# ScalarE's order in an attention slot: the exponential ahead of the value copy and of the transposed-row copy

## The chip, the cores and the metric

The kernel runs on one core of one Trainium2 chip. The metric is device time in microseconds of one execution of the whole kernel; the lower the better. Times of several executions are summed up by their median.

## What is computed

The kernel is one transformer block on 16 batches of 256 tokens with 256 features, all in float32 at the interface:

```python
q = (layernorm(x) @ Wq_w + Wq_b)                      # 16 heads of 16 features
k = (ctx @ Wk_w + Wk_b); v = (ctx @ Wv_w + Wv_b)
scores = where(mask == 0, -1e9, q @ k.T / sqrt(16))
x = x + softmax(scores) @ v @ Wo_w + Wo_b
h = layernorm(x)
# feed-forward: 8 experts, the 2 best of each token, weighted by softmax(h @ gate_w.T)
out = sum over the 2 experts of w * ((silu(g) * u) @ down) + sigmoid(h @ sg) * shared_mlp(h)
return x + out
```

## The kernel before

**Stages.** The program has an attention stage (up to about 395 us of the profile; it also computes the router and rounds the expert weights into pairs of 16-bit parts), and a feed-forward stage that begins to fill TensorE towards the end of the first. The change is in the first alone.

**Slots.** Attention is a software pipeline written out by hand: iterations `i` of 8 slots `u`, the same nested loop in the instruction stream of each engine. In every slot TensorE issues, in this order: the scores S of one unit (batch `i-1`, unit `u`; a unit is a query half and a group of 4 heads' pairs; lines 1101 masks and 1120 products), the ring work of the slot, the transposed scores T of one unit of an earlier batch (lines 1101 and 1136), and in every other slot the product with the values PV (line 1152). S units go to one PSUM pair `ps_st`, T units to the other. VectorE takes the row maximum of each S (line 994); ScalarE takes the exponential of each T (line 803). The next S waits for the maximum of the last S, and the next T waits for the exponential of the last T, because each pair is used again at once (`wait_pair`).

**The ring.** Projections and transposes share two PSUM banks `ps_m` in turn. The steady order of a period is: slot 0 `mt` (transposed maxima, line 1281) and `rt` (router, line 1418), slot 1 `xt`, slot 2 `ct` (transposes, line 1162), slot 3 `q`, slot 4 `k` (projections, line 1175), slot 5 `v` (value projection, line 1311), slot 6 `ht` (transposes of the normalised rows of batch `i-5`, line 1409), slot 7 `o` (output projection, line 1251). Whoever writes a bank waits until its last user has freed it, so `o` waits for the copy of `v`, and `mt` for the copy of `ht`.

**ScalarE.** In slot 5 ScalarE before the change waits for the value projection, makes two copies of it into `vx` (line 776, 128x256 each), waits for their own semaphore, frees the bank, and then waits for the T unit of the slot and takes its exponential (line 803). In slot 6 it does the same with one copy of the transposed rows into `hT` (line 745, 128x1024 of 16 bits) ahead of the exponential. From slot 4 it carries two copies of the attention output out of `ps_o` (lines 814 and 815) and two DMA issues for the sums (line 377, `sums_across`). The first of the copies waits until GpSimd has divided the outputs of the batch before (line 655, semaphore `s_n`). The buffer `vx` has three parts, used by batch modulo 3; PV of a batch needs its values two iterations after they are projected. The rows `hT` are read by the router in slot 0 of the next iteration and by a DMA (line 824) that ScalarE issues after the exponential of slot 7.

**Other queues.** SyncE's queue carries, in order, the load of the context, the loads of expert weights (line 498), the writes (519) and reads (531, 532) of `q` and `k` through DRAM, and the joining of the sums (383), which waits for the sums DMA of ScalarE. In iterations 5 to 9 there is a second load of expert weights behind the join. GpSimd rounds the weights (631, 638), scatters rows (1393) and divides (655, 663). On VectorE slots 5 and 6 hold the routing chain (1334 to 1348), the maximum of S, the normalisation (871, 877), and in slot 7 a reciprocal (935), a maximum, and the residual add (1010).

Below, units are named by slot: T5 is the T unit of slot 5, PE issues it behind the value projection; T6 is that of slot 6 and waits for the exponential of T5; S7 is the scores unit of slot 7.

Of the kernel before, what the change touches and what calls it, by code (L numbers as in the profile page):

```python
# [5 lines left out]
FP16 = mybir.dt.float16  # L6
# [8 lines left out]
D = 256  # L15
NB = 16
# [149 lines left out]
def attention(nc, sb, sem, xr, fwh, fwl, ident, moe, x, ctx, mask, w_in, bias_in, w_o, ffn_in, gate_in, ident_in,  # L166
# [4 lines left out]
    with ExitStack() as here:  # L171
# [131 lines left out]
        def now(kind, i, u):  # L303

            return [b for b in range(NB) if when.get((kind, b)) == 8 * i + u]
# [121 lines left out]
        def taken(i, u, kind):  # L427

            g = 8 * i + u
            found = filler.get(g - 1) if g <= LAST_T + 1 else filler.get(g)  # L430
            return found[1:] if found and found[0] == kind else None
# [253 lines left out]
        def _(eng):  # L685
# [24 lines left out]
            def shared_high(n, c):  # L710
# [7 lines left out]
                    eng.wait_ge(s_st, 8 * (NB - 1)) if n else eng.wait_ge(s_v, NB)  # L718
                eng.activation(f_hi[n % 2][rows, c, :], hf[k % 2][rows, :], ACT.Copy).then_inc(moe.f_hh, 1)

            eng.wait_ge(s_anyb, 1)
            eng.activation(anyr[:, :], bank("any")[:, 0:SEQ], ACT.Copy).then_inc(s_any33, 1)
            eng.wait_ge(s_any33, 1)
# [3 lines left out]
            for i in range(ITER):  # L727
                for u in range(8):
# [8 lines left out]
                        eng.wait_ge(s_small, 64)  # L737
                        eng.activation(gh[:, :, :], g32[:, :, :], ACT.Copy).then_inc(s_gh, 1)
                    for kind, b in uses(i, u):
                        if kind == "ht":  # L740
                            eng.wait_ge(s_ht, b + 1)
                            if b:
                                eng.wait_ge(s_rt, b)
                                eng.wait_ge(s_tw, 16 * b)
                            eng.activation(hT[:, :, :, :].rearrange("p l c t -> p (l c t)"),
                                           bank((kind, b))[:, :].bitcast(FP16), ACT.Copy).then_inc(s_th, 1)
                            eng.wait_ge(s_th, b + 1)
                            eng.nop().then_inc(free((kind, b)), 1)
                        elif kind == "mt":
                            eng.wait_ge(s_mt, b + 1)  # L750
                            if b:
                                eng.wait_ge(s_mw, 16 * b)
                            eng.activation(nm[:, :], bank((kind, b))[0:H, 0:SEQ], ACT.Copy, scale=-1.0).then_inc(s_nm, 1)
                            eng.wait_ge(s_nm, b + 1)
                            eng.nop().then_inc(free((kind, b)), 1)
                        elif kind in ("xt", "ct"):
                            s_in, dst, s_out, s_used = (s_xt, xT[0], s_xh, s_q) if kind == "xt" else (s_ct, cT[0], s_ch, s_v)
                            eng.wait_ge(s_in, b + 1)
                            if b:
                                eng.wait_ge(s_used, b)  # L760
                            eng.activation(dst[:, :], bank((kind, b))[:, :], ACT.Copy).then_inc(s_out, 1)
                        elif kind in ("q", "k"):
                            s_in, dst, s_out, s_used = (s_q, qhl, s_qh, s_qw) if kind == "q" else (s_k, khl, s_kh, s_kw)
                            eng.wait_ge(s_in, b + 1)
                            if b:
                                eng.wait_ge(s_used, 16 * b)
                            eng.activation(dst[:, :, 0, :], bank((kind, b))[:, :].rearrange("p (h t) -> p h t", h=2),
                                           ACT.Copy).then_inc(s_out, 1)
                        elif kind == "v":
                            eng.wait_ge(s_v, b + 1)  # L770
                            if b == 0:
                                eng.wait_ge(s_const, 7)
                            if b >= 3:
                                eng.wait_ge(s_pv, 4 * (b - 2))
                            for tt in range(TT):
                                last = eng.activation(vx[b % 3][:, tt, :, 0:DK],
                                                      bank((kind, b))[:, tt * D:(tt + 1) * D].rearrange("p (h d) -> p h d", h=H),
                                                      ACT.Copy)
                                last.then_inc(s_vx, 1)
                            eng.wait_ge(s_vx, 2 * b + 2)  # L780
                            eng.nop().then_inc(free((kind, b)), 1)  # L781
                    if (i, u) == (0, 2):
                        eng.wait_ge(s_bias, 32)
                        eng.wait_ge(s_ones, 1)
# [11 lines left out]
                    if st:  # L796
                        n = 8 * st[0] + st[1]
                        eng.wait_ge(s_st, n + 1)
                        if n >= 4:
                            eng.wait_ge(s_pv, (n - 4) // 2 + 1)  # L800
                        if n == 3:
                            eng.wait_ge(s_gl, 1)
                        eng.activation(expo[n % 4][:, :, :], ps_st[pair["T", n]][:, :].rearrange("p (h q) -> p h q", h=4), ACT.Exp,  # L803
                                       scale=SCALE).then_inc(s_e, 1)
                    if taken(i, u, "up"):
                        shared_high(*taken(i, u, "up"))
                    if pv and pv[1] == 7:
# [1183 lines left out]
```

## Time and profile before

| what | value |
|---|---|
| median of 3 runs | 814.75 us |
| the runs | 810.08, 815.7, 814.75 us |
| span of the profiled execution | 811.5 us |
| time of the profiled execution apart from its span | not listed |
| TensorE busy | 744.4 us, 92% of the span |
| ScalarE busy | 397.1 us, 49% |
| VectorE busy | 547.1 us, 67% |
| GpSimd busy | 340.9 us, 42% |
| mean granted TensorE clock | 0.977 of full |

The span runs from the first to the last instruction of one profiled execution. It lies inside the range of the three timed runs.

### The profile page before, as it was taken

The page shows a single profiled execution, that of the slowest core. Times are in us where ns is not written, and L with a number is a line of the kernel's source. Part 1 is how long each engine was busy: PE and PEld are TensorE (multiplying, and loading weights), DVE is VectorE, ACT ScalarE, POOL GpSimd, SP SyncE. Part 2 cuts the span into 40 slices and gives each one's busy share as a digit, 9 for nine tenths or more (in the row PEclk, how much of TensorE's full clock was granted, in tenths as well). Part 3 has the DMA queues.
Part 4 walks back from the last instruction along what each step waited for, and adds up shares of the span by engine and source line. Part 5 has one row for each costly group of instructions (what it writes and reads, how often), then busy time and mean ns, then how long its engine had stood idle before and what let it go on. Part 6 is the DMA issues. An engine that isn't in the chain of part 4 may idle for free.

```text
span 811.5 us, 21926 instructions
## 1 busy us (share of the span) xinstructions
PE 744.4 (92%) x8123; PEld 464.9 (57%) x8123; DVE 547.1 (67%) x1174; ACT 397.1 (49%) x679; POOL 340.9 (42%) x499
## 2 busy tenths in 40 slices
PE   5689899989988999998989978999999999999997
PEld 4445455545555555554454654677777777655555
DVE  6675677978988998888765678533333333358797
ACT  4124556655655666666555462344444444433231
POOL 6131144586676665555403232011121121267773
PEclk9878999999999999999999999999999999999999
DMA  6643555655554554545512213488888988834743
GB/s 185 174 135 122 169 153 168 184 157 164 158 140 139 165 152 150 155 132 162 152 42 75 86 60 111 102 168 176 168 164 175 162 165 172 153 115 124 234 148 113
DMA packets 164234, 118.26 MB, mean 146 GB/s; under 512 B 108450, under 2 KB 143522, under 8 KB 164132
## 3 DMA queue, kind: packets, MB, share of 16 engines
q1 hardware_dynamic: 146564, 82.44, 41.3%
q0 software_dynamic: 9552, 26.10, 10.7%
q10 hardware_dynamic: 8016, 8.33, 3.3%
q8 instruction: 69, 1.13, 0.6%
q14 instruction: 33, 0.27, 0.1%
HBM read 52.78 MB, written 38.14 MB: 112 GB/s over the span
## 4 chain that ended last, share of the span: by engine, by line
PE 52%; DVE 14%; DMA 9%; POOL 7%; ACT 7%; issue 6%; SPq 4%; ACTq 1%; DVEq 0%; POOLq 0%
PE ps_st L1889 15%; PE ps_m L1904 8%; PE ps_st L1461 5%; PE ps_st L1101 5%; DVE mx L994 4%; PE ps_o L1152 4%; PE ps_m L1175 3%; POOL p L1670 2%; POOL expert_rows L1393 2%; DMA arena<-ffn_dram 2%; PE ps_st L1120 2%; PE ps_m L1251 2%; ACT p L803 2%; PE ps_o L1472 1%; DMA qk_scratch<-arena 1%
## 5 line engine op out<-in xcount | busy, mean ns | idle before, releaser
L994 DVE TENSOR_REDUCE mx<-ps_st 128x4 f32<-128x1024 f32 x128 | 155.7, 1217 | 40.2 <-PE ps_st L1120 32.5
L803 ACT ACTIVATE p<-ps_st 128x1024 f32<-128x1024 f32 x128 | 131.0, 1023 | 75.8 <-PE ps_st L1136 68.1
L1889 PE MATMUL ps_st<-fwh,p 128*128 x568 | 137.9, 313 | 1.1 <-DMA p<-expert_rows 1.1
L1662 POOL DMA_DIRECT2D sorted_out<-p x71 | 38.6, 543 | 180.7 <-ACT p L1719 177.0
L1393 POOL DMA_INDIRECT expert_rows<-hrow,slot x64 | 64.7, 1011 | 59.4 <-DVE slot L1384 38.7
L1889 PE MATMUL ps_st<-fwl,p 128*128 x284 | 88.8, 313 | 0.0
L1889 PEld LDWEIGHTS ps_st<-fwh,p 128*128 128x128 f16 x568 | 55.5, 98 | 28.3 <-issue 2.0
L1101 PE MATMUL ps_st<-maskq,identb 64*64 64x512 bf16 x512 | 53.8, 410 | 19.5 <-DVE mx L994 15.3
L1101 PE MATMUL ps_st<-mb_k,identb 64*64 64x512 bf16 x256 | 52.4, 406 | 18.9 <-ACT p L803 18.1
L1461 PE MATMUL ps_st<-qk,arena 128*128 128x512 f16 x264 | 61.1, 386 | 3.3 <-DVE qk L913 1.8
L1461 PE MATMUL ps_st<-q,arena 128*128 128x512 f16 x264 | 59.7, 379 | 3.2 <-DVE qk L913 2.2
L1719 ACT ACTIVATE p<-ps_m 128x256 f32<-128x256 f32 x71 | 27.2, 383 | 69.8 <-PE ps_m L1904 67.2
L1670 POOL DMA_INDIRECT p<-sorted_out,xn x52 | 53.0, 1019 | 17.8 <-issue 14.6
L631 POOL CAST fwh<-arena 128x272 f16<-128x272 f32 x80 | 33.5, 459 | 63.3 <-DMA arena<-ffn_dram 63.3
L1811 DVE TENSOR_TENSOR qk<-ps_st,maskq 128x352 f32<-128x352 f32 x36 | 18.9, 524 | 60.5 <-PE ps_st L1889 60.3
L1811 DVE TENSOR_TENSOR qk<-ps_st,vx 128x352 f32<-128x352 f32 x35 | 18.4, 524 | 59.8 <-PE ps_st L1889 59.8
L1175 PE MATMUL ps_m<-arena 128*128 128x256 f16 x256 | 54.2, 285 | 0.5 <-ACTq L781 0.4
L638 POOL TENSOR_TENSOR fwl<-arena,fwh 128x272 f16<-128x272 f32 x80 | 54.2, 710 | 0.6
L1101 PE MATMUL ps_st<-turned_k,identb 64*64 64x512 bf16 x256 | 52.4, 406 | 0.0
L1152 PE MATMUL ps_o<-p,vx 128*17 128x256 f32 x704 | 48.7, 396 | 0.0
L1101 PEld LDWEIGHTS ps_st<-maskq,identb 64*64 64x64 bf16 x512 | 14.7, 105 | 56.8 <-DVE mx L994 36.9
L1461 PEld LDWEIGHTS ps_st<-qk,arena 128*128 128x128 f16 x264 | 25.3, 99 | 34.7 <-issue 3.0
(237 smaller groups left out, 1750.4 us busy)
## 6 DMA issues: line engine op xcount, KB each, us to landing
arena<-ffn_dram SPq DMA_DIRECT2D x20, 544.0 KB
sorted_out<-p POOLq DMA_DIRECT2D x71, 128.0 KB, 2.9
qk_scratch<-arena SPq DMA_DIRECT2D x32, 256.0 KB, 2.9
qk<-qk_scratch SPq DMA_DIRECT2D x44, 128.0 KB, 3.0
arena<-ctx_dram SPq DMA_DIRECT2D x16, 256.0 KB, 3.8
hT_dram<-hT ACTq DMA_DIRECT2D x16, 256.0 KB, 2.5
out_dram<-xr SPq DMA_DIRECT2D x16, 256.0 KB, 2.9
xr<-x_dram SPq DMA_DIRECT2D x7, 512.0 KB, 4.2
```

Source lines behind the costliest of these rows:

```text
L638: last = eng.tensor_tensor(lo[:, cols], aw32[:, cols], hi[:, cols], ALU.subtract)
L803: eng.activation(expo[n % 4][:, :, :], ps_st[pair["T", n]][:, :].rearrange("p (h q) -> p h q", h=4), ACT.Exp, scale=SCALE).then_inc(s_e, 1)
L994: eng.tensor_reduce(mx[b % 2][:, qt, :].rearrange("p (h g j) -> p h g j", h=2, g=HG)[:, :, hg, :], ps_st[pair["S", 8 * b + n]][:, :].rearr ...
L1101: mm(ps[to, 2 * hh * SEQ:2 * (hh + 1) * SEQ], identb[rows, rows], bias[rows, :].unsqueeze(1).broadcast_to([64, 2, SEQ]), start=True, stop= ...
L1152: last = mm(ps_o[32 * j:32 * j + DK + 1, hg * SEQ:(hg + 1) * SEQ], vx[b % 3][:, kt, 4 * hg + j, :], expo[(8 * b + 2 * hg + kt) % 4][:, 2 * ...
L1175: mm(oo, w[:, at:at + P], srcT[xl][:, dc * SEQ:(dc + 1) * SEQ], start=dc == 0 and (wl, xl) == TERMS[0], stop=False)
L1393: eng.indirect_dma_start(expert_rows, bass.IndirectOffsetOnAxis(moe.slot[:, j, n:n + 1], 0), hrow[:, tt, :], None).then_inc(moe.s_sc[b % 3 ...
L1461: last = eng.matmul(o[:, :], moe.sw[:, wl, at:at + P], moe.hT[blk % 2][:, :, xl, dc, :], start=dc == 0 and (wl, xl) == (0, 0), stop=dc == ...
L1662: eng.dma_start(sorted_out[k * P:(k + 1) * P, :], ys[k % 3][:, :]).then_inc(r_st[k % 3], 16)
L1670: eng.indirect_dma_start(ya[n % NGB][:, j, :], None, sorted_out, bass.IndirectOffsetOnAxis(packed[:, j, n:n + 1], 0)).then_inc(r_ga[n % NG ...
L1889: last = mm(o[:, 0:INTER], xgT[k % NXG][:, xl, dc, :], (fwh, fwl)[wl][:, bass.ds(e, 1), w0 + dc * INTER:w0 + (dc + 1) * INTER], start=dc = ...
L1904: last = mm(ps_d[2 + b % 2][:, 0:D], turned(b)[:, xl, c, :], (fwh, fwl)[wl][:, bass.ds(e, 1), at:at + D], start=c == 0 and (wl, xl) == (0, ...
```

## The change

In slots where batch 3 or a later one has its value projection, the two copies of the values, with the wait for the projection and the release of the bank, move behind the exponential of the slot. In iterations below 16 the copy of the transposed rows, with its waits and its release, moves behind the exponential of its slot too. Batches 0 to 2 keep the old order for the values, and iterations 16 on keep it for the rows (batch 11 and later). No instruction is added or removed; the two blocks became functions. The DMA issues of ScalarE and its other work keep their places behind both.

```diff
+            def values_out(b):
+                eng.wait_ge(s_v, b + 1)
+                ...
+                if b >= 3:
+                    eng.wait_ge(s_pv, 4 * (b - 2))
+                for tt in range(TT):
+                    last = eng.activation(vx[b % 3][:, tt, :, 0:DK], ..., ACT.Copy)
+                    last.then_inc(s_vx, 1)
+                eng.wait_ge(s_vx, 2 * b + 2)
+                eng.nop().then_inc(free(("v", b)), 1)
+
+            def turned_rows_out(b):
+                eng.wait_ge(s_ht, b + 1)
+                if b:
+                    eng.wait_ge(s_rt, b)
+                    eng.wait_ge(s_tw, 16 * b)
+                eng.activation(hT[:, :, :, :].rearrange("p l c t -> p (l c t)"),
+                               bank(("ht", b))[:, :].bitcast(FP16), ACT.Copy).then_inc(s_th, 1)
+                eng.wait_ge(s_th, b + 1)
+                eng.nop().then_inc(free(("ht", b)), 1)
...
                     for kind, b in uses(i, u):
-                        if kind == "ht":
-                            ...
+                        if kind == "ht" and i >= NB:
+                            turned_rows_out(b)
...
-                        elif kind == "v":
-                            ...
+                        elif kind == "v" and b < 3:
+                            values_out(b)
...
                         eng.activation(expo[n % 4][:, :, :], ps_st[pair["T", n]][:, :].rearrange("p (h q) -> p h q", h=4), ACT.Exp,
                                        scale=SCALE).then_inc(s_e, 1)
+                    for b in now("v", i, u):
+                        if b >= 3:
+                            values_out(b)
+                    for b in now("ht", i, u):
+                        if i < NB:
+                            turned_rows_out(b)
                     if taken(i, u, "up"):
```

## Rows read from the trace of the kernel before

**Rows 1.** The page: the chain that ended last, shares by engine

```profile
PE 52%; DVE 14%; DMA 9%; POOL 7%; ACT 7%; issue 6%; SPq 4%; ACTq 1%; DVEq 0%; POOLq 0%
```

**Rows 2.** Waits of TensorE, 80 to 375 us: total, times, longest

```profile
PE ps_st L1101 <- ACT p L803: 16.6, 14, 3.7
```

**Rows 3.** Timeline of batch 12's slots: start, length, engine, line, idle before

```profile
298.87 0.39 PE L1136 MATMUL ps_st<-qk 49*64 49x256 f16 x8
298.95 0.66 ACT L776 ACTIVATE vx<-ps_m 128x256 f32<-128x256 f32 x2 [0.78 <-PE ps_m L1311]
...
299.80 1.02 ACT L803 ACTIVATE p<-ps_st 128x1024 f32<-128x1024 f32 x1 [0.19 <-ACT vx L776]
...
300.71 1.02 ACT L745 ACTIVATE hT<-ps_m 128x1024 f16<-128x1024 f16 x1
300.83 1.21 DVE L994 TENSOR_REDUCE mx<-ps_st 128x4 f32<-128x1024 f32 x1
...
300.87 0.40 PE L1101 MATMUL ps_st<-mb_k,identb 64*64 64x512 bf16 x2 [0.62 <-ACT p L803]
...
302.42 0.41 PE L1101 MATMUL ps_st<-maskq,identb 64*64 64x512 bf16 x4
...
303.29 1.16 DVE L994 TENSOR_REDUCE mx<-ps_st 128x4 f32<-128x1024 f32 x1
...
304.61 0.41 PE L1101 MATMUL ps_st<-mb_k,identb 64*64 64x512 bf16 x2
304.72 0.69 DVE L1010 TENSOR_TENSOR xr<-ps_m,xr 128x512 f32<-128x512 f32 x1 [0.27 <-PE ps_m L1251]
```

**Rows 4.** The chain that ended last, 40 to 400 us: start, length, what

```profile
81.78 0.67 ACT vx L776 x2
...
201.22 3.58 DMA sums<-odd
...
367.52 0.67 ACT vx L776 x2
```

**Rows 5.** Timeline of batch 7's slots 4 to 7, from 174 us

```profile
174.67 0.60 ACT L814 ACTIVATE oj<-ps_o 128x512 f32<-128x512 f32 x1 [3.08 <-POOL rb L655]
...
177.04 0.66 ACT L776 ACTIVATE vx<-ps_m 128x256 f32<-128x256 f32 x2 [0.77 <-issue]
177.89 1.02 ACT L803 ACTIVATE p<-ps_st 128x1024 f32<-128x1024 f32 x1 [0.19 <-ACT vx L776]
...
178.96 0.40 PE L1101 MATMUL ps_st<-mb_k,identb 64*64 64x512 bf16 x2 [3.71 <-ACT p L803]
...
184.28 0.40 PE L1101 MATMUL ps_st<-mb_k,identb 64*64 64x512 bf16 x2
```

**Rows 6.** Timeline: T5 and T6 of batch 3, T6 of batches 4, 9 and 10

```profile
81.15 0.39 PE L1136 MATMUL ps_st<-qk 49*64 49x256 f16 x8
...
83.70 0.40 PE L1101 MATMUL ps_st<-mb_k,identb 64*64 64x512 bf16 x2 [1.72 <-ACT p L803]
...
106.49 0.40 PE L1101 MATMUL ps_st<-mb_k,identb 64*64 64x512 bf16 x2 [1.17 <-ACT p L803]
...
229.36 0.40 PE L1101 MATMUL ps_st<-mb_k,identb 64*64 64x512 bf16 x2 [2.50 <-ACT p L803]
...
253.83 0.40 PE L1101 MATMUL ps_st<-mb_k,identb 64*64 64x512 bf16 x2 [2.05 <-ACT p L803]
```

**Rows 7.** Stretches: length, busy of five engines, granted TensorE clock, DMA, GB/s

```profile
86.00:88.00 2.00, 1.92 (x28) 0.92 (x24) 0.78 (x1) 0.03 (x1) 0.00 (x0) 0.58 0.26 57
...
181.00:183.00 2.00, 2.00 (x21) 1.02 (x18) 0.77 (x1) 0.03 (x1) 0.39 (x1) 0.50 0.46 68
...
226.00:232.00 6.00, 3.50 (x65) 1.87 (x58) 5.47 (x15) 4.28 (x7) 5.33 (x10) 1.00 0.63 140
...
256.00:258.00 2.00, 2.00 (x18) 1.07 (x11) 1.13 (x1) 0.00 (x0) 0.21 (x1) 0.50 0.22 49
```

**Rows 8.** Batch 13: the first scores unit of the next iteration

```profile
328.43 0.41 PE L1101 MATMUL ps_st<-maskq,identb 64*64 64x512 bf16 x4 [0.45 <-DMA qk<-qk_scratch]
```

More of the change, by code:

```diff
@@ L719, in shared_high @@
                 eng.activation(f_hi[n % 2][rows, c, :], hf[k % 2][rows, :], ACT.Copy).then_inc(moe.f_hh, 1)
+            def values_out(b):
+                eng.wait_ge(s_v, b + 1)
+                if b == 0:
+                    eng.wait_ge(s_const, 7)
+                if b >= 3:
+                    eng.wait_ge(s_pv, 4 * (b - 2))
+                for tt in range(TT):
+                    last = eng.activation(vx[b % 3][:, tt, :, 0:DK],
+                                          bank(("v", b))[:, tt * D:(tt + 1) * D].rearrange("p (h d) -> p h d", h=H),
+                                          ACT.Copy)
+                    last.then_inc(s_vx, 1)
[10 more added lines that the diff above has]
+                eng.nop().then_inc(free(("ht", b)), 1)
             eng.wait_ge(s_anyb, 1)
@@ L739, in _ @@
                     for kind, b in uses(i, u):
-                        if kind == "ht":
[L741 to L748, printed above, removed]
+                        if kind == "ht" and i >= NB:
+                            turned_rows_out(b)
                         elif kind == "mt":
@@ L768, in _ @@
                                            ACT.Copy).then_inc(s_out, 1)
-                        elif kind == "v":
[L770 to L781, printed above, removed]
+                        elif kind == "v" and b < 3:
+                            values_out(b)
                     if (i, u) == (0, 2):
```

## The prediction

> **What bounds the kernel now.** I read the page first. Its busy times say that TensorE is occupied for 92% of the span (the table above has it), and the chain by engine gives it only 52%, with 7% on ScalarE [rows 1]. So the end is set by TensorE with hand-overs to the other engines in between, and an edit of ScalarE's order can pay only at such a hand-over. The second view is the waits of TensorE in the stretch where the edit acts: 16.6 us of idle time before a T unit ended with an exponential, 14 times, the longest 3.7 us [rows 2]. These 16.6 us are the whole pot in which the change can fish. The third view is the timeline of one ordinary batch, and it shows where in the period the hand-over is: T6 starts at 300.87 after 0.62 us of idle time, right behind the end of T5's exponential at 299.80 + 1.02 = 300.82 [rows 3]. That exponential was itself late: T5's last products end at 298.87 + 0.39 = 299.26, but ScalarE was in the two value copies until 298.95 + 0.66 = 299.61 and then waited 0.19 us for its own semaphore [rows 3]. The fourth view is the chain that ended last. It passes through the value copies of eight batches, the first at 81.78 (batch 3) and the last at 367.52 (batch 15); the others are 4, 7, 10, 11, 12 and 14 [rows 4]. It goes round those of 5, 6, 8, 9 and 13, by a DMA or by SyncE's queue, as at 201.22 where the sums transfer of batch 8 carries it [rows 4].
>
> **The value copies, in ordinary batches (4, 11, 12, 14, 15).** Nothing is added or removed; two copies, one self-wait and one release go from before the exponential to behind it. In batch 12 the exponential would start when T5 has landed, estimated at 299.26 + 0.05 = 299.31 (the 0.05 is a hand-over between the two engines: in batch 7 the exponential ended at 178.91 and TensorE went on at 178.96 [rows 5]). Before, it started at 299.80, so it is 0.49 us earlier, and T6 starts at 300.38 with 0.13 us of idle time left [rows 3]. Does the 0.49 reach the end? First limit: S7 needs the maximum of S6, which VectorE begins only at 300.83, behind its routing chain, and ends at 302.04 [rows 3]. S7 stood at 302.42, so it can come 0.33 earlier (302.04 + 0.05 = 302.09), and then VectorE is late, not ScalarE. Second limit: the residual add at 304.72 waited 0.27 us for TensorE; VectorE is free for it at 303.29 + 1.16 = 304.45 [rows 3]. From there the chain runs on VectorE (the add, statistics, the maximum of the next S). So 0.27 us of the 0.49 are kept. Bounds: zero, if a loop beside this chain is just behind it, and 0.49. I take 0.27, since it is read off a row. Five batches: 5 x 0.27 = 1.35 us.
>
> **The value copies where GpSimd held ScalarE (batches 7 and 10).** In batch 7 ScalarE stood for 3.08 us before a slot 4 copy until GpSimd had divided [rows 5]. T5 was complete long before, so here the exponential takes the place of the value copies at once: 177.04 in place of 177.89, which is 0.85 us, and the pause of TensorE before T6 falls from 3.71 to 2.86 [rows 5]. No limit behind it is near: T6 comes so late there that VectorE has long ended the maximum of S6. Batch 10 has the same pattern with a pause of 2.05 us [rows 6]. Two batches: 1.70 us. Batch 9 has it too (2.50 us [rows 6]) but the chain goes round it: GpSimd, the sums transfer and the next load of expert weights form a loop of their own there, and an earlier T6 only lengthens the next pause. I count nothing for 8 and 9.
>
> **Batch 3.** ScalarE came to the value copies only at 81.78 [rows 4], later than T5 ended (81.15 + 0.39 = 81.54 [rows 6]), so the exponential takes their place at once and again the whole 0.85 us is won. Its pause of 1.72 us [rows 6] becomes 0.87.
>
> **Batches 5, 6 and 13.** After batch 13 the first scores unit waited 0.45 us for the read of q and k from DRAM [rows 8]. That transfer starts from slot 3 and 4, ahead of the edit. A T6 that comes 0.3 us earlier only lengthens this wait. Nothing for these three.
>
> **The transposed rows.** The copy of 1.02 us at 300.71 ran before T6's exponential, which waited for it until 301.91 [rows 3]. Now the exponential starts at about 301.2 and the copy ends near 303.3 in place of 301.73. The next T unit, which needs that exponential, comes at 304.61 [rows 3], so the gain is worth nothing. The delay is covered as well: the bank goes to the transposed maxima and the rows to the router, both behind 304.61, so about 1.3 us of cover are left. The DMA of the rows is issued after the exponential of slot 7, behind 305, and is not moved. If that cover were gone the cost would be up to the 1.02 + 0.19 us of the copy and its wait in each of the 11 iterations.
>
> **What the later value copies cost.** They now end at 300.34 + 0.66 = 301.0, and the bank is free at about 301.2 in place of 299.8. Who is queued for it is the output projection, behind S7 at 302.42, or at 302.09 when S7 comes earlier [rows 3]: at least 0.9 us of cover. In batch 7 the release comes near 178.9 and that projection stands beyond 181, so there is more. PV of that batch comes two iterations later. ScalarE's DMA issues of slot 4 stand ahead of slot 5 and are not moved, those of slot 7 stand behind its exponential; SyncE's and GpSimd's queues are passed by nothing. Taken at zero.
>
> **TensorE's clock.** Behind the pause of batch 7 the granted clock fell: 0.50 of full, the 1.2 GHz level, from 181 to 183, and T6 to the next T took 184.28 - 178.96 = 5.32 us [rows 5, 7] against 304.61 - 300.87 = 3.74 in batch 12 [rows 3]. One such fall costs 1.58 us. A fall came after the pauses of 3.71, 2.05 and 1.72 us (0.50, 0.50 and 0.58 of full), and none after that of 2.50 (1.00) [rows 5 to 7]. So a shorter pause may avoid it, but the length alone doesn't decide. I take the falls of 7 and 10 as kept, since the one pause stays long and the other is lengthened again by what batch 9 gives it, and that of batch 3 as gone, since its pause is halved. There I count 0.4 us, not 1.58, because the next scores then wait for the reads of q and k. Bounds of this term: 0 to 2 x 1.58 + 0.4 = 3.6 us in favour, and as much against if other pauses are now followed by a fall. The Trainium skill (TensorE: Matmul & The Clock Gate, section "What's actually happening") says that the gate judges recent activity over a window that runs freely and is not started by the kernel; by this rule the 2.50 us pause without a fall beside the 2.05 us one with a fall is a matter of phase, and every shift of the schedule draws anew. The sum by it would be the same 3.9 us plus or minus a draw; the trace agrees as far as these four pauses go.
>
> **Sum.** 1.35 + 1.70 + 0.85 + 0.4 = 4.3 us, 0.5% of the span of 811.5. The profiled execution's time apart from its span isn't listed; the span lies inside the three runs (810.08 to 815.7), 3.25 below their median. I subtract from the median: 814.75 - 4.3 = 810.4 us. The shift should reach the end, since the chain behind attention is TensorE for most of its length.
>
> **Rivals.**
> First, the gain is lost: the chain goes through the value copies only by small margins, and the loops beside it (SyncE's reads and weight loads, GpSimd's rounding) are a fraction of a microsecond behind, as in 5, 6, 8, 9 and 13. For it: rows 8, and the loop in batches 8 and 9. Against it: batches 11, 12 and 14 repeat without any such wait. If only 3, 7 and 10 pay half, 1.3 us: 813.5.
> Second, the gain is larger, because the clock no longer falls after batches 7 and 10: 4.3 + 2 x 1.58 = 7.5 us: 807.3. For it: the pause of 2.05 us gets shorter. Against it: 2.86 us is still long. To get over 1%, which is 8.1 us and about what a measurement of this kernel can tell from no change, this would have to come with the full 0.49 in the ordinary batches (5 x 0.22 = 1.1 more): 806.2.
> Third, it becomes slower: the clock falls more often. The place is the pauses before T6 that remain (batches 4, 7, 8, 9, 10), the price is 1.58 us for each new fall, and it decides from three new falls on, since 3 x 1.58 = 4.7 is more than 4.3. Four new ones: 814.75 - 4.3 + 6.3 = 816.8. For it: a fall came after 1.72 us but not after 2.50, and batch 4's pause of 1.17 isn't much shorter [rows 6]. Against it: all pauses get shorter or stay.
> Fourth, the change doesn't do what it says: in one place the exponential isn't earlier, since T5 lands after the value copies. In batch 12 T5 ended at 299.26 and the copies at 299.61 [rows 3], so this holds only if TensorE gets later relative to ScalarE: 814.75.
>
> **How the numbers follow.** Forecast 0.52; gain lost 0.20; larger 0.15; slower 0.08; without effect 0.05. The range reaches to the larger case's 806.2 and takes in the lost and the void one: 805.5 to 815.5, since the three runs alone lie 5.6 apart. Faster by over 1% (below 806.6): 0.10. Slower by over 1% (above 822.9): 0.03. Within 1%: 0.87.
>
> **What would show it.** In the timeline of the changed kernel the exponential of T5 starts within 0.1 us of the end of T5 and the value copies follow; the idle time before T6 is 0.1 to 0.2 us in ordinary batches, and in batches 7 and 10 about 0.85 less than before if their length is otherwise kept. The exponentials' share in TensorE's waits falls from 16.6 us to about 9. S7 begins within 0.1 us of the end of S6's maximum. In the chain the pair of value copy and exponential is replaced by the maximum of S6. The granted clock from 84 to 88 us stays at 1.00. The forecast is wrong if the output projection or the router waits for a ScalarE copy, if the ordinary batches keep their period, or if falls of the clock multiply.

## The result, and the profile after

| | before | after |
|---|---|---|
| median of 16 runs each, taken together | 810.01 us | 803.25 us |
| lowest and highest run | 807.02, 815.7 | 800.67, 809.49 |
| profiled execution: its time, its span | not listed, 811.5 | 800.67, 798.5 |
| mean granted TensorE clock | 0.977 | 0.984 |

The ratio is 0.9911, 95% interval 0.9892 to 0.9931: 0.9% faster, 7.2 us of 810. The same kernel measured a second time (e8 below) gave 0.9937 [0.991, 0.9963], 5.1 us. The gain is therefore told as 5 to 7 us, from two measurements whose intervals together reach from 3 to 9 us. The forecast was 4.3 us of gain and 810.4 us; the time fell outside its range on the fast side. The two profiled executions lie 13.0 us apart, about twice the gain of the medians, so they can't be subtracted from each other as they stand. This is taken up below.

First the chain that ended last, by engine, as the page of the changed kernel has it:

```profile
PE 48%; DVE 25%; issue 7%; DMA 7%; POOL 6%; ACT 4%; SPq 2%; DVEq 0%; ACTq 0%; POOLq 0%
```

Against [rows 1] ScalarE fell from 7% to 4% and VectorE rose from 14% to 25%: the hand-over that the edit shortened is now passed on VectorE. TensorE's waits from 80 to 375 us say the same (total, times, longest):

```profile
PE ps_st L1115 <- DVE mx L1008: 8.2, 22, 1.4
PE ps_st L1115 <- ACT p L811: 6.9, 5, 2.9
PE ps_st L1115 <- DMA qk<-qk_scratch: 1.6, 3, 1.0
```

The 16.6 us in 14 waits of [rows 2] became 6.9 in 5. Next, the timeline of batch 12, which answers to [rows 3]:

```profile
287.94 0.39 PE L1150 MATMUL ps_st<-qk 49*64 49x256 f16 x8
...
288.38 1.02 ACT L811 ACTIVATE p<-ps_st 128x1024 f32<-128x1024 f32 x1 [1.14 <-PE ps_st L1150]
288.58 2.68 POOL L638 TENSOR_TENSOR fwl<-arena,fwh 128x272 f16<-128x272 f32 x4
...
288.73 0.59 DVE L1359 TENSOR_TENSOR chosen<-which,table 128x32 f32<-128x32 uint32 x1
289.30 0.66 ACT L729 ACTIVATE vx<-ps_m 128x256 f32<-128x256 f32 x2
289.36 0.61 DVE L1362 TENSOR_TENSOR sel<-chosen 128x16 f16<-128x16 f32 x1
...
289.45 0.40 PE L1115 MATMUL ps_st<-mb_k,identb 64*64 64x512 bf16 x2
...
289.89 1.21 DVE L1008 TENSOR_REDUCE mx<-ps_st 128x4 f32<-128x1024 f32 x1
...
291.06 1.02 ACT L742 ACTIVATE hT<-ps_m 128x1024 f16<-128x1024 f16 x1
291.16 0.41 PE L1115 MATMUL ps_st<-maskq,identb 64*64 64x512 bf16 x4
...
292.35 1.16 DVE L1008 TENSOR_REDUCE mx<-ps_st 128x4 f32<-128x1024 f32 x1
...
293.35 0.41 PE L1115 MATMUL ps_st<-mb_k,identb 64*64 64x512 bf16 x2
293.46 0.69 DVE L1024 TENSOR_TENSOR xr<-ps_m,xr 128x512 f32<-128x512 f32 x1
```

T5 ends at 287.94 + 0.39 = 288.33 and its exponential starts 0.05 later; the value copies follow; T6 starts at 289.45 with no idle time, 0.05 behind the exponential. S7 starts 0.06 behind the end of S6's maximum (289.89 + 1.21 = 291.10), and the residual addition no longer waits for TensorE: it starts right behind VectorE's own maximum, where it waited 0.27 us before. The copy of the rows ends at 292.08, with 1.27 us left until T7. From residual addition to residual addition an ordinary batch takes 22.40 us in place of 22.72 to 22.75. (Batch 14, with a wait for the read of q and k in it, takes 22.59 in place of 23.13.)

The places with a pause, in batches 3, 7, 9 and 10, answer to [rows 5] and [rows 6]:

```profile
79.21 0.40 PE L1115 MATMUL ps_st<-mb_k,identb 64*64 64x512 bf16 x2 [0.87 <-ACT p L811]
...
168.16 0.60 ACT L828 ACTIVATE oj<-ps_o 128x512 f32<-128x512 f32 x1 [3.07 <-POOL rb L655]
...
170.53 1.02 ACT L811 ACTIVATE p<-ps_st 128x1024 f32<-128x1024 f32 x1 [0.77 <-issue]
171.45 0.66 ACT L729 ACTIVATE vx<-ps_m 128x256 f32<-128x256 f32 x2
171.60 0.40 PE L1115 MATMUL ps_st<-mb_k,identb 64*64 64x512 bf16 x2 [2.86 <-ACT p L811]
...
176.92 0.40 PE L1115 MATMUL ps_st<-mb_k,identb 64*64 64x512 bf16 x2
...
220.72 0.41 PE L1115 MATMUL ps_st<-mb_k,identb 64*64 64x512 bf16 x2 [1.64 <-ACT p L811]
...
244.80 0.40 PE L1115 MATMUL ps_st<-mb_k,identb 64*64 64x512 bf16 x2 [1.32 <-ACT p L811]
...
248.55 0.40 PE L1115 MATMUL ps_st<-mb_k,identb 64*64 64x512 bf16 x2
```

The pauses before T6 were 1.72, 3.71, 2.50 and 2.05 us and are 0.87, 2.86, 1.64 and 1.32. In 3 and 7 that is 0.85 less each, the length of the value copies with their wait, as forecast. The stretches, whose last figures are granted clock, DMA share and GB/s, show what the clock did behind batches 3 (first two rows), 7 and 10, against [rows 7]. The fall of batch 3 stood 2.3 us behind the start of its T6 before (83.70), so it is to be looked for from 81 us on, and not only from 84:

```profile
81.00:83.00 2.00, 1.02 (x28) 0.63 (x24) 1.22 (x1) 1.02 (x1) 0.00 (x0) 1.00 0.33 84
84.00:88.00 4.00, 3.82 (x70) 1.87 (x63) 2.65 (x4) 2.70 (x4) 0.00 (x0) 1.00 0.45 139
172.00:174.00 2.00, 2.00 (x40) 0.73 (x28) 0.35 (x1) 1.82 (x3) 2.00 (x4) 0.73 0.17 53
174.00:176.00 2.00, 2.00 (x17) 1.20 (x10) 1.23 (x1) 0.22 (x1) 0.79 (x2) 0.50 0.22 49
246.00:250.00 4.00, 4.00 (x69) 2.58 (x62) 3.79 (x7) 2.19 (x3) 1.96 (x4) 1.00 0.24 53
```

Behind batch 7 it still fell to 0.50, the 1.2 GHz level, and T6 to T7 took 176.92 - 171.60 = 5.32 us, as before. Behind 3 and 10 it stayed at 1.00: T6 to T7 took 2.01 us in batch 3 (before 3.26) and 3.75 in batch 10 (before 5.31).

**Where the profile pair's 13.0 us lie.** Subtracting the starts of the residual additions gives a shift that grows step by step. 3.64 us of it stood already at 68 us, ahead of the first instruction that the edit moves, under the same instruction order in both kernels: that part isn't the change's. (The first residual addition comes in batch 4's slots, so the part of batch 3 is read from TensorE's next S units: 88.59 and 82.81, a shift of about 5.8.) From there to 361 us the shift grows by 8.80 to 12.44, and then it stays, to the last addition of attention at 455.83 (12.47). So what was won in attention did reach the end. By batches:

| batches | forecast | grown in the pair |
|---|---|---|
| 3 | 0.85 + 0.4 | 2.15 |
| 4, 11, 12, 14, 15 | 1.35 | 1.99 |
| 7, 10 | 1.70 | 0.43 + 1.95 |
| 5, 6, 13 | 0 | 1.01 |
| 8, 9 | 0 | 0.33 + 0.94 |
| sum | 4.3 | 8.80 |

### The profile page after: what moved, and what is told of

Read it like the earlier page. It is cut to its first block, busy times and chain, and to the rows that moved or that the text cites. A ratio compares the mean times of both kernels' runs of the same rounds, so it can differ in the third digit from the quotient of the medians.

```text
span 798.5 us, 21926 instructions
## 1 busy us (share of the span) xinstructions
PE 739.3 (93%) x8123; PEld 463.8 (58%) x8123; DVE 548.0 (69%) x1174; ACT 395.8 (50%) x679; POOL 339.5 (43%) x499
## 4 chain that ended last, share of the span: by engine, by line
PE 48%; DVE 25%; issue 7%; DMA 7%; POOL 6%; ACT 4%; SPq 2%; DVEq 0%; ACTq 0%; POOLq 0%
PE ps_st L1903 16%; DVE mx L1008 9%; PE ps_m L1918 8%; PE ps_st L1475 5%; PE ps_st L1115 4%; POOL p L1684 3%; PE ps_o L1166 2%; DMA qk_scratch<-arena 2%; PE ps_m L1189 2%; POOL expert_rows L1407 2%; PE ps_st L1134 2%; PE ps_o L1486 1%; DVE arena L1064 1%; PE ps_m L1486 1%; DVE arena L1058 1%
## 5 line engine op out<-in xcount | busy, mean ns | idle before, releaser
L1733 ACT ACTIVATE p<-ps_m 128x256 f32<-128x256 f32 x71 | 27.2, 383 | 69.5 <-PE ps_m L1918 67.0
L1475 PEld LDWEIGHTS ps_st<-qk,arena 128*128 128x128 f16 x264 | 25.4, 99 | 35.1 <-issue 3.9
```

What stands on the lines that cost most here:

```text
L1475: last = eng.matmul(o[:, :], moe.sw[:, wl, at:at + P], moe.hT[blk % 2][:, :, xl, dc, :], start=dc == 0 and (wl, xl) == (0, 0), stop=dc == ...
```

## The experiments

Each builds on the changed kernel. In all, the two conditions (`b >= 3` for the values, `i < NB` for the rows) are written as lists of batches, which give the changed kernel for 3 to 15 and 0 to 10. Ratios are to the kernel before on the same chip; it had a median of 811.54 us on the chip of e1 to e4, 853.27 on that of e5 to e7, 810.34 on that of e8 to e11 and 812.14 on that of e12. Each experiment has one profiled execution.

**e1_values_only and e2_rows_only: one part alone.**

```diff
-ROWS_LATE = tuple(range(0, 11))      # e1
+ROWS_LATE = ()
-VALUES_LATE = tuple(range(3, 16))    # e2
+VALUES_LATE = ()
```

> Only the value copies (batches 3 to 15) go behind the exponential; the transposed rows keep the old order. Theory A (all of the gain comes from an earlier exponential of T5; the rows' order is worth nothing because T7 comes more than 3 us later): the whole gain of the change stays, 6 to 8 us, ratio 0.990 to 0.993, and in batch 12 TensorE waits at most 0.15 us before T6. Theory B (the rows' order carries a part, by freeing T6's exponential or by unloading VectorE's and ScalarE's PSUM reads): at least 2 us of the gain are missing, ratio 0.994 or above.

> Only the copy of the transposed rows (batches 0 to 10) goes behind its exponential; all value copies keep the old order. Theory A: nothing, within 1 us of the kernel before, ratio 0.999 to 1.001, and in batch 12 T6 still waits 0.62 us. Theory B: 2 us or more faster, ratio 0.9975 or below. If the later release of the bank or of the rows holds the router up, it is slower by up to 1.2 us in each of 11 iterations.

Measured: e1 0.9916 [0.9884, 0.9948], e2 0.9991 [0.996, 1.0023]. The values alone carry the whole gain, as theory A has it. The rows alone do nothing that can be seen: the interval would hide up to 3 us, but in e2's profile the ordinary batches keep their 22.7 us (two of them have 23.1, like batch 14 before) and T6 of batch 12 still waits 0.63 us.

**e3_ordinary and e4_held: the values in two groups of batches.**

```diff
+VALUES_LATE = (4, 5, 6, 8, 11, 12, 13, 14, 15)   # e3
+VALUES_LATE = (3, 7, 9, 10)                      # e4
```

> Value copies go behind the exponential only in the batches where ScalarE wasn't held before them (4, 5, 6, 8, 11 to 15), rows as in the change. Theory A: about 0.33 us for each of the ordinary batches that lie on the chain, the limit being VectorE's maximum of S6; 7 to 9 of them, 2.3 to 3.0 us, ratio 0.996 to 0.997; the pauses of batches 3, 7, 9, 10 keep their length (1.7, 3.7, 2.5, 2.0 us). Rival (the gain is mostly the ordinary batches, my 0.27 us having been too low because the limit behind it moves too): 5 us or more, ratio 0.994 or below.

> Value copies go behind the exponential only in batches 3, 7, 9 and 10, where the exponential could take their place at once; rows as in the change. Theory A: 0.85 us in each of 3, 7 and 10 and, where the shorter pause spares a fall of TensorE's clock, 1.25 us (batch 3) and 1.56 us (batch 10) more: 2.5 us if no fall is spared, 5.4 us if both are, ratio 0.997 to 0.993; the granted clock behind batch 10's pause is 1.00. Rival (the falls are chance and don't hang on the length of these pauses): 2.5 us, ratio 0.997, with falls in some pauses of this profile as in the one before.

Measured: e3 0.9973 [0.9942, 1.0004], e4 0.9953 [0.9923, 0.9983], 2.2 and 3.8 us. e4 alone is clear of no change; e3 isn't. Together they make 0.74%, near e1's 0.84%. Both lie in theory A's ranges. e3 has the short period (22.41) in batches 11, 14 and 15 (12 and 13 take 23.07, which is taken up under e8), and yet in batch 7 this:

```profile
174.09 0.64 PE L1117 MATMUL ps_st<-mb_k,identb 64*64 64x512 bf16 x2 [4.20 <-ACT p L813]
...
180.20 0.40 PE L1117 MATMUL ps_st<-mb_k,identb 64*64 64x512 bf16 x2
```

The pause that was 3.71 us is 4.20 there: TensorE comes earlier, GpSimd's division doesn't, and 0.49 us of what batches 4 to 6 won is given back. The fall behind it cost more too (6.11 us from T6 to T7). The pauses of batches 9 and 10 did not keep their length either: they were 2.02 us, now with a fall (T6 to T7 5.18), and 0.60, without one.

**e5_route_later: VectorE's routing of batches 0 to 9 a slot later,** so that S6's maximum no longer stands behind it.

```diff
+when.update({("route", b): 8 * (b + 6) + 6 for b in range(10)})
```

> The changed kernel, and VectorE's routing chain of batches 0 to 9 goes from slot 5 to slot 6, behind the maximum of S6 in place of ahead of it. Theory A (after the change VectorE is the limit of the ordinary batches: the maximum of S6 waits for the routing chain, and S7 for that maximum): S7 no longer waits, up to 0.16 us more in each of 10 iterations, but the chain's 2.2 us still stand before the maximum of S7 and the residual add; so between 1.6 us faster and 1 us slower than the change alone, ratio to the kernel before 0.989 to 0.9925. Rival (VectorE isn't the limit, the hand-over of T6 still is): ratio as the change's 0.991 within 0.0005 and S7 stands where it stood. If the chain now delays the residual add by its whole length, up to 2 us in each iteration are lost and the kernel is slower than before.

Measured: 0.9998 [0.997, 1.0026], so it loses the gain, as the last sentence of the expectation feared. The distance between residual additions of batches 11 to 14 is 25.4 to 25.8 us, but for one of 27.2, with 24.5 for e6 on that chip. S7's wait is gone, but the addition now comes 1.53 us behind T7 in place of 0.11, since the routing stands ahead of it, and other maxima are late: from 80 to 400 us TensorE waits for maxima 33 times, 15.9 us in all, where e6 has 21 and 9.7. The profiled execution was one of e5's longest (860.58 us, median 853.15), so the 0.9 to 1.3 us of the distances are no typical size; the ratio doesn't rest on it.

**e6_keep_busy and e9_busy_once: no fall of the clock by keeping TensorE busy.** In the pause TensorE repeats the transposes of slot 6 (the same result again): in e6 for three batches, in e9 for the iteration of batch 7 alone.

```diff
-transpose_rows(eng, moe, bank((kind, b)), hrow[b % 3]).then_inc(s_ht, 1)
+for _ in range({2: 5, 4: 3, 5: 3}.get(b, 0)):    # e6; e9: 3 if b == 2 else 0
+    transpose_rows(eng, moe, bank((kind, b)), hrow[b % 3])
+transpose_rows(eng, moe, bank((kind, b)), hrow[b % 3]).then_inc(s_ht, 1)
```

> The changed kernel, and TensorE repeats the transposes of the rows in the pauses before T6: 5 more times for the rows of batch 2 (pause of value batch 7, 2.86 us), 3 more times for those of 4 and 5 (batches 9 and 10, 1.64 and 1.32 us). The repeats write the same values to the same bank. Theory A (the clock falls behind a pause because TensorE did too little before): with about 0.45 us for each repeat the clock behind batch 7's pause stays at 1.00, T6 to T7 takes 3.9 us in place of 5.3, and 1.4 to 1.6 us are gained on the change: ratio 0.989 to 0.9905 to the kernel before. Rival (falls come by chance or by something else, such as power or a fixed time in the kernel): the fall behind batch 7 stays, T6 to T7 is 5.3 us, ratio as the change's.

> The changed kernel, and TensorE repeats the transposes of the rows 3 more times in the pause before T6 of value batch 7 alone (about 0.45 us each, inside a pause of 2.86 us, so that T6 isn't delayed). Theory A (the fall behind that pause is caused by TensorE's idleness): T6 to T7 takes 3.75 to 3.9 us in place of 5.3, the clock from there on is 1.00, and 1.4 us are gained on the change, ratio lower by 0.0017. Rival (the fall comes whatever TensorE does there): 5.3 us again, ratio as e8's.

Measured: e6 0.9936 [0.9904, 0.9967], e9 0.9941 [0.9912, 0.9971]; the change itself has 0.9937 on e9's chip. In both profiles the fall of batch 7 is gone (T6 to T7 3.75 and 3.74). e9's stretches there:

```profile
170.00:172.00 2.00, 1.39 (x28) 0.63 (x28) 1.35 (x3) 1.82 (x4) 2.00 (x4) 1.00 0.41 119
172.00:174.00 2.00, 2.00 (x30) 1.42 (x25) 1.16 (x1) 1.23 (x2) 1.80 (x4) 1.00 0.22 49
```

The total shows nothing of it, so the first half of theory A held and its gain didn't. In e6 the repeats were too many: T6 of batches 9 and 10 started 1.2 us behind the end of T5's exponential. In e9, T6 to T7 of batch 9 took 8.01 us in place of 3.74, for another reason:

```profile
215.13 1.29 POOL L665 TENSOR_TENSOR onl<-rb,onh 128x256 f16<-128x256 f32 x2
215.28 3.84 DVE L1354 TENSOR_TENSOR sc<-ex,tot 128x16 f32<-128x16 f32 x1
216.39 2.67 POOL L640 TENSOR_TENSOR fwl<-arena,fwh 128x272 f16<-128x272 f32 x4
...
220.15 1.22 DVE L1010 TENSOR_REDUCE mx<-ps_st 128x4 f32<-128x1024 f32 x1
...
221.42 0.41 PE L1117 MATMUL ps_st<-maskq,identb 64*64 64x512 bf16 x4 [3.04 <-DVE mx L1010]
```

A routing operation of 16 elements a partition, usually 0.28 us, took 3.84, and its end (219.12) is that of GpSimd's row of subtractions (219.06). The maximum behind it is late, and S7 waits 3.04 us. The loss isn't 4.3 us, though: in return the pause of batch 9 is 0.49 us in place of 1.64 and that of batch 10 is gone, so the two batches take 50.20 us together, against 48.72 in the first profile of the change. And over batches 7 to 10 e9 takes 98.79 us against 98.91, in spite of the fall that it was spared. e4 has 98.73 there and no profile has less. So something behind TensorE seems to hold these four batches together; which engine it is was not tried here.

**e7_values_slot6 and e10_values_slot6_again: the value copies still later,** behind the exponential of slot 6. This tests how much cover the ring leaves.

```diff
-for b in now("v", i, u):
-    if b in VALUES_LATE:
+for b in range(NB):
+    if when.get(("v", b)) == 8 * i + u - 1 and b in VALUES_LATE:
```

> The changed kernel, and the value copies of batches 3 to 15 move one slot further, behind the exponential of T6. This takes the cover of the bank's release away. Theory A (the cover is about 0.9 us before the output projection): the bank is free near 0.85 us after the end of T6's exponential, some 0.3 us later than the output projection wants it, so that projection waits for a ScalarE copy and 0.2 to 0.4 us are lost in each of 8 to 10 batches: 2 to 4 us slower than the change, ratio 0.993 to 0.996. Rival (the output projection has slack of its own, since VectorE is the limit now): ratio as the change's 0.991.

> The changed kernel with the value copies behind the exponential of T6, one slot further, now beside the change on one chip. Theory A (the later value copies cost nothing as long as the bank is free before the output projection; at 2.7 us after T5's exponential they end just as it comes): within 1 us of e8, the output projection starts at most 0.1 us later. Rival (the bank's release has less cover than the trace shows): 2 us or more slower than e8.

Measured: e7 0.9914 [0.9885, 0.9942], e10 0.9936 [0.9909, 0.9963], the latter beside 0.9937 for the change on that chip. In e7 the output projection is now behind the copies, by hardly anything:

```profile
305.21 0.66 ACT L731 ACTIVATE vx<-ps_m 128x256 f32<-128x256 f32 x2
...
305.96 0.10 PEld L1263 LDWEIGHTS ps_m<-bhl,tri 128*128 128x128 f16 x1 [0.25 <-ACTq L736]
```

So the cover of the ring was real: a further slot of delay costs nothing that the total can show. It isn't nothing in the profiles: T6 to T7 takes 3.99 us in both, against 3.90 in e8 and 3.94 in e6 on the same chips, and an undisturbed batch of e10 takes 22.50 us where the change has 22.40, so the cover ends here.

**e8_change_again: the changed kernel once more.**

> The changed kernel itself once more, beside the three that follow, since the last three ran on a chip where the kernel before takes 853 us. Theory A (the gain is made of ScalarE's hand-overs and of spared falls of the clock, which any chip has): ratio 0.989 to 0.993. Rival (part of the gain belongs to the chip or to the state in which the program starts): ratio above 0.995.

Measured: 0.9937 [0.991, 0.9963], 804.7 us beside 810.34, between the two theories' ranges, and its interval takes in parts of both. In its profile batch 10 pauses for 2.38 us and the clock falls behind it (T6 to T7 5.31), where the first profile had 1.32 and no fall; batch 7 pauses for 3.36. Batches 12 and 14 take 23.06 and 24.19 us where the first profile had 22.40 and 22.59:

```profile
291.60 0.64 DVE L1352 TENSOR_TENSOR sc<-ex,tot 128x16 f32<-128x16 f32 x1
...
295.40 0.41 PE L1117 MATMUL ps_st<-maskq,identb 64*64 64x512 bf16 x4 [0.74 <-DVE mx L1010]
...
321.81 0.41 PE L1117 MATMUL ps_st<-maskq,identb 64*64 64x512 bf16 x4 [1.18 <-DMA qk<-qk_scratch]
```

The routing operation `sc` took 0.64 us in place of 0.28, since it started beside another of GpSimd's operations (see the last section), and S7 waited 0.74 us for the maximum behind it. Such batches of 0.66 us more, with T6 to T7 at 4.56, come seven times in the profiles of e1, e3, e8 and e10, six of them with a `sc` of 0.58 to 0.65, and not at all in the first profile. In batch 14 the read of q and k was 1.18 us late on top, where the first profile had 0.23. From the addition of batch 4 to that of batch 15 the same program took 256.78 us in one execution and 261.40 in the other.

**e11_outputs_behind: in iterations 7, 9 and 10 the output copies, the sums DMAs and the copy for the division go behind the exponential of slot 5,** so that it no longer waits for GpSimd.

```diff
-if pv and pv[1] == 7:
+if pv and pv[1] == 7 and i not in (7, 9, 10):
     outputs_out(pv[0])
...
+if i in (7, 9, 10) and u == 5:
+    outputs_out(units(i, 4)[2][0])
+    divide(i, 4)
```

> A version built on the reading that the pauses left before T6 (2.86, 1.64 and 1.32 us in batches 7, 9 and 10) come from ScalarE standing in its slot 4 copies until GpSimd has divided: in iterations 7, 9 and 10 those copies, the copy of the divided outputs and the two DMA issues go behind T5's exponential too. Theory A: T6 no longer pauses there, TensorE stops later at PV, which needs the outputs out of PSUM, but T6 and its exponential are done by then; 1.0 to 2.5 us in batch 7, 0.5 to 1.5 in 9 and 10, and the fall behind batch 7 may go (1.5 more): 2 to 5 us faster than e8, ratio 0.984 to 0.989. Rival (GpSimd's loop sets the pace there, so a pause moves from T6 to PV one for one): within 1 us of e8.

Measured: 0.992 [0.9886, 0.9954], 805.12 us, not clearly better than the change's 0.9937, and short of theory A. The pauses of 7, 9 and 10 are gone, and two costs stand in their place. In batch 7:

```profile
173.58 0.40 PE L1129 MATMUL ps_st<-mb_k,identb 64*64 64x512 bf16 x2
...
174.65 1.06 PE L1180 MATMUL ps_o<-p,kv 128*17 128x256 f32 x16 [0.44 <-ACT odd L732]
...
176.72 0.27 PE L1275 MATMUL ps_m<-bhl,tri 128*128 128x256 f16 x1 [0.45 <-POOL onl L665]
```

T6 starts unhindered, but PV waits for the bank of the outputs and the output projection for GpSimd: T6 to T7 takes 4.76 in place of 3.74. And batch 8, which had no pause, now has the one that batch 7 lost:

```profile
196.61 0.60 ACT L731 ACTIVATE oj<-ps_o 128x512 f32<-128x512 f32 x1 [3.06 <-POOL rb L657]
...
200.06 0.57 PE L1129 MATMUL ps_st<-mb_k,identb 64*64 64x512 bf16 x2 [2.85 <-ACT p L841]
```

Over batches 7 to 10 this profile (one of the longer executions, 809.34 us) takes 105.08 us, against 102.03 in e8. So the wait for GpSimd's division only moved to the next batch: ScalarE's order chose where TensorE stands still for it, here at a worse place.

**e12_routing_split: e9 with the last two operations of VectorE's routing (`chosen`, `sel`) behind the maximum of S6,** in the routing of batches 0 to 9.

```diff
-for _ in route(eng, link, moe, b, s_sel):
-    pass
+pieces = route(eng, link, moe, b, s_sel)
+next(pieces)
+next(pieces)
+halfway.append(pieces)
...
+if u == 6 and halfway:
+    for _ in halfway.pop():
+        pass
```

> The change with the repeats of e9_busy_once for rows of batch 2, and in the routing of batches 0 to 9 VectorE's last two operations of the chain (chosen, sel) are issued behind the maximum of S6 in place of before it. Theory A, VectorE's maximum is now the end that TensorE waits for in the ordinary batch: S7's wait for S6's maximum (0.16 us after the change) goes, the distance between residual additions of ordinary batches falls from 22.40 to between 22.1 and 22.25, and the ratio to before is 0.988 to 0.992. Theory B, VectorE's work per batch is the limit whatever its order: the distance stays 22.40 and the ratio is as e9_busy_once's, 0.993 to 0.995. In either case a stall of some us in one batch, as the 3.84 us operation of e9_busy_once, stays possible where VectorE's operations stand beside GpSimd's.

Measured: 0.9911 [0.9881, 0.9941], 803.32 us, on another chip than e9. The interval takes in e9's ratio and both theories'. The profile tells more. VectorE in the ordinary batch there:

```profile
291.19 0.64 DVE L1364 TENSOR_TENSOR sc<-ex,tot 128x16 f32<-128x16 f32 x1
...
292.55 1.22 DVE L1011 TENSOR_REDUCE mx<-ps_st 128x4 f32<-128x1024 f32 x1
...
293.87 1.04 DVE L893 TENSOR_SCALAR xn<-xr,mv,rsa 128x256 f32<-128x256 f32 x2
294.95 0.19 DVE L1373 TENSOR_TENSOR chosen<-which,table 128x32 f32<-128x32 uint32 x1
295.18 0.17 DVE L1376 TENSOR_TENSOR sel<-chosen 128x16 f16<-128x16 f32 x1
...
295.53 1.16 DVE L1011 TENSOR_REDUCE mx<-ps_st 128x4 f32<-128x1024 f32 x1
296.61 0.67 DVE L1027 TENSOR_TENSOR xr<-ps_m,xr 128x512 f32<-128x512 f32 x1
```

S7's wait is gone (T6 to T7 3.74 in place of 3.90), but the distance is 22.35 to 22.36, only 0.05 less than 22.40. The two moved operations became short (0.19 and 0.17 in place of 0.59 and 0.61), but in this batch `sc` took 0.64 in place of 0.28 and the normalisation 1.04 in place of 0.73, and the maximum of S7 and the addition still stand in a row behind them. The first half of theory A held, its gain didn't: in this part of the period VectorE's sum counts, as theory B has it. The stalled operation came again in batch 9 (3.83 us), and so did the clock's fall behind batch 7, after a pause of 2.00 us, in spite of the repeats.

## Why the prediction was wrong, step by step

The mechanism was right. Three terms were mis-sized: the base that the gain was subtracted from (4.74 us too high), the clock (0.4 us, where the profile pair has 2.8 and the average over executions about 1.3), and the batches that were given nothing (2.28 us in the pair). They stand one by one below, with two smaller ones.

**The base.** Of the 7.15 us between the forecast and the median, 4.74 are the step "I subtract from the median: 814.75". That was the middle of three runs 5.6 us apart; 16 runs have 810.01. The ratio that the forecast implies, 0.53% off, lies just outside the interval of the first measurement (0.69% to 1.08%) and inside that of the repeat (0.37% to 0.90%).

**The direction, the mechanism and the place were right.** The exponential of T5 starts 0.05 us behind T5, T6 has no idle time in ordinary batches, the waits for exponentials fell from 16.6 to 6.9 us (forecast about 9; 9.3 in e8), no engine waits for a moved copy, and the values alone give the whole effect (e1, e2, e7, e10). The other 2.4 us are sizes.

**Ordinary batches, forecast 0.27 us each: 0.33.** The second limit of this step was VectorE, "free at 304.45", the recorded end of the maximum. The addition begins 0.05 before that end (293.46 against 292.35 + 1.16 = 293.51), so the limit was 0.32. e3 has the same 22.41. That VectorE sets this end now was argued then; e12 supports it.

**Batches 5, 6, 8, 9 and 13, forecast nothing: 2.28 us in the profile pair.** The step was that a loop beside the chain takes each gain back. For batches 5 and 8 this is no draw: they take 22.20 to 22.22 and 22.92 to 22.94 us in the profiles of the change, of e1, e3 and e8, and 22.80 to 22.82 and 23.25 in those of the kernel before, of e2 and e4, where these batches keep the old order. For batch 13 it named the read of q and k. After the change the first scores unit there waits 0.23 us for the read, not the 0.45 of [rows 8] plus 0.3, and the batch is 0.33 shorter. A rest of a loop in one batch isn't proof of a loop that runs at the same pace; for that the waits would have had to grow from batch to batch. The chains that ended last show what the read hangs on: in both kernels it starts behind VectorE's work that follows the residual addition of batch 12, so it isn't beside the chain but a branch of it, and moves with what was won before. From that addition to the first scores unit it is 23.71 us before and 23.16 after; 0.53 of the 0.55 are the read itself (3.64 and 3.11 us in the chain), which is a draw: in e8 the unit waited 1.18 us.

**Batch 7, forecast 0.85: the pause fell by 0.85 but the shift grew by only 0.43.** The step "no limit behind it is near" overlooked the limit ahead: GpSimd's division. It ended 18.41 us behind the last addition in place of 17.98, so 0.43 us of what 4 to 6 had won was given back. e3 shows the same by itself (4.20 in place of 3.71). e11 tried to get round it by ScalarE's order and didn't.

**The clock: forecast 0.4 us for the fall of batch 3, none for that of batch 10.** In the profile pair this is the largest miss. The first came to 1.25 us (3.26 - 2.01; with the pause that is 2.10 of the 2.15), so the discount for the reads of q and k was wrong: the wait for them is there (0.98 us at 82.81), but the kernel before waited 0.67 us for a maximum at the same place. Not all of this fall is the shorter pause's, either: e3 keeps the pause of 1.72 us and had no fall behind it (T6 to T7 2.01). The second came to 1.56 in the first profile and to nothing in the repeat's. The forecast had both inside its bounds for the term (0 to 3.6). My second rival, 7.5 us, is nearer to the first measurement's 7.2, by one of its two falls and for the rest by luck; the repeat's 5.1 is nearer to the 4.3. The draw between executions is visible: the changed kernel, unchanged, has a pause of 1.32 with no fall once and of 2.38 with a fall once. That this accounts for the difference between 7.2 and 5.1 us is argued, since only one execution of each was profiled. The size on average can be told better, since every execution has its mean granted clock. Leaving out the chip of e5 to e7, it is 0.9801 on average over 93 executions of the kernel before and of e2, 0.9783 over 12 of e3, and 0.9822 over 94 of the kernels that have the values late in batches 3, 7, 9 and 10 (the same without e9 and e12); the standard errors are 0.0004, 0.0009 and 0.0003. Among executions of one kernel a clock higher by 0.001 goes with a time shorter by 0.6 us. So the clock's part of the gain is some 1.3 us, an estimate from these figures: more than the 0.4 of the forecast and less than the 2.8 of the profile pair. It also says that e3's order alone brings no such part.

**What stays open.** How often the falls of batches 7 and 10 in particular, and the stalled operation of batch 9, come in executions that weren't profiled. e9, e11 and e12 show no version that is certainly faster than the change: their ratios of 0.9941, 0.992 and 0.9911 lie within its own two.

## What to carry to other kernels

When an engine frees a buffer for later and produces something that the bottleneck waits for now, let it do the second first, and find how late the buffer may come: here a further slot of delay cost 0.1 us a batch. Count the gain in the ordinary period by the next engine's slack (0.3 of 0.5 us), ask of a wait beside the chain whether it branches off the chain and so moves with it, and look ahead of each held place for the engine that holds it, because it takes back what the batches before it won. And take the base from as many runs as there are: three runs 5.6 us apart can't carry a forecast of a 4 us gain.

## What the runs showed of the hardware

**Short operations of VectorE beside GpSimd's.** In batch 12 above, `chosen` took 0.59 us and `sel` 0.61, while four GpSimd subtractions of 2.68 / 4 = 0.67 us each ran; away from them, in e12, the same operations took 0.19 and 0.17. Each seems to last until the GpSimd operation that was running has ended (288.58 + 0.67 = 289.25; `chosen` ends at 289.32). The `sc` of 0.64 us in e8 is of this kind too: it started at 291.60 beside a GpSimd subtraction that ended about 292.21, and ended at 292.24; in the first profile it took 0.28, since the subtraction beside it was near its end. The Trainium skill (SBUF — State Buffer, section "SBUF: two separate sides") has an exclusive lock on ports that the two engines share, for VectorE operations with two inputs in SBUF as these are: whichever starts first keeps them for its whole instruction and the other stands. The trace agrees with that for the operations of 0.6 us. It doesn't explain the 3.84 us of e9: that operation began 0.15 us after the first of two GpSimd subtractions and ended only behind the last of the four that followed them, so it stood through about six instructions, not one. It came in three of the kernels (e9, e10, e12: 3.84, 3.84, 3.83 us, always in batch 9 and the `sc` operation). S7 waits about 3 us for it each time; what it costs in the end is less, as e9's two batches show.

**Pauses and the clock.** In the profiles of the chips on which the kernel before takes some 810 us, no pause before T6 of up to 1.65 us was followed by a fall. Of those from 1.71 us on, most were (1.71, 1.72, 2.00, 2.02, 2.05, 2.38, 2.85 and all longer ones), but not 1.72 in e3, 2.03 in e2 and 2.50 before: so the length of the pause alone doesn't decide. Behind batch 3 the clock fell in 2 of the 3 profiles with the old order there (before, e2, e3; pauses of 1.71 and 1.72 us) and in none of the 8 with the new one (0.86 to 0.89 us). A fall lengthens T6 to T7 by 1.1 to 2.4 us.

**The chip.** The kernel before took 853.27 us on the chip of e5 to e7 and 810.01 to 812.14 on the others. The profile of e6 shows ordinary batches of the kind that take 22.4 us taking 24.5, and waits of TensorE on its own issue that the other chips' profiles don't have there:

```profile
312.83 0.41 PE L1117 MATMUL ps_st<-maskq,identb 64*64 64x512 bf16 x4 [0.73 <-issue]
```

This wait is a third of the 2.1 us by which such a batch is longer; the rest wasn't followed. Ratios agreed between the chips (0.9914 and 0.9936 for the same edit, e7 and e10), times don't.
